# One causal attention layer of a decoder: both norms worked by batches inside the attention's stage, and the reciprocals of the softmax sums on ScalarE as exponential of the logarithm

## The reference, cut to what matters

```
x = x + L3_attn(layernorm(x))            # the first norm has no gain and no bias

def L3_attn(x, Wq, bq, Wk, bk, Wv, bv, Wo, bo, gamma, beta):      # 16 heads of 8
    q, k, v = heads(x @ Wq + bq), heads(x @ Wk + bk), heads(x @ Wv + bv)
    att = softmax(where(causal, q k^T / sqrt(8), -inf))
    y = merge(att v) @ Wo + bo
    return (y - mean(y)) / sqrt(var(y) + 1e-5) * gamma + beta     # the output norm
```

## Time and profile before

| | |
|---|---|
| median of 3 runs | 2105.82 us |
| profiled execution | 2109.4 us, span 2107.6 us, mean granted clock 0.949 |
| TensorE matmul, weight load | 1887.7 us (90%), 1342.2 us (64%) |
| VectorE, ScalarE, GpSimd | 1378.9 us (65%), 1159.7 us (55%), 897.8 us (43%) |
| `L2624` maxima, VectorE, in the layer | 57.3 us of 48 and 37.1 us of 32 |
| `L2607` exponentials, ScalarE, in the layer | 31.0, 24.4, 17.4 and 10.7 us, 32 of each width |
| `L2644` RECIPROCAL, VectorE | 26.9 us of 8, 3357 ns each |

### The profile page before, as it was taken

One profiled execution on the slowest core, in us unless ns is written; L12 is line 12 of the kernel. 1 busy time (PEld: TensorE's weight loads), 2 busy tenths in 40 slices (PEclk: granted clock), 3 DMA queues, 4 the chain that ended last, 5 costly groups with the idle time before them and its releaser, 6 DMA issues. The chain is left out here.

```text
span 2107.6 us, 50657 instructions
## 1 busy us (share of the span) xinstructions
PE 1887.7 (90%) x20016; PEld 1342.2 (64%) x20016; DVE 1378.9 (65%) x2444; ACT 1159.7 (55%) x2448; POOL 897.8 (43%) x1143
## 2 busy tenths in 40 slices
PE   7888999987568999999999877999899989999786
PEld 4336778853345788888888744888788856633332
DVE  4446788865944777777785334888777758934434
ACT  4555555555757666656664344555455551066453
POOL 0003445520625677666764201676566640044200
PEclk9999999999569999999999898999999999999898
DMA  6000100100003000000000042444344410000100
GB/s 290 1 1 2 61 30 31 41 1 0 1 0 151 33 14 23 14 23 14 23 17 20 23 181 53 123 130 135 108 127 127 130 41 2 1 1 1 37 1 21
DMA packets 31950, 107.00 MB, mean 51 GB/s; under 512 B 9440, under 2 KB 9568, under 8 KB 30816
## 3 DMA queue, kind: packets, MB, share of 16 engines
q1 hardware_dynamic: 30624, 103.58, 14.6%
q10 hardware_dynamic: 1088, 0.13, 0.0%
HBM read 93.67 MB, written 10.03 MB: 49 GB/s over the span
## 5 line engine op out<-in xcount | busy, mean ns | idle before, releaser
L762 PE MATMUL bank<-yh,wl 128*128 128x512 f32 x640 | 253.7, 396 | 11.7 <-issue 5.8
L763 PE MATMUL bank<-yl,wh 128*128 128x512 f32 x640 | 251.5, 393 | 0.0
L764 PE MATMUL bank<-yh,wh 128*128 128x512 f32 x640 | 251.5, 393 | 0.0
L2294 DVE SCALAR_TENSOR_TENSOR big<-bank,pack,big 128x256 f32<-128x256 f32 (+2 forms) x384 | 182.8, 477 | 40.2 <-ACT mask L2184 22.8
L1757 DVE TENSOR_TENSOR hl<-bank,hh 128x512 fp32r<-128x512 f32 x192 | 132.7, 691 | 69.3 <-ACT hh L1690 59.9
L2183 ACT ACTIVATE big<-bank,pack 128x256 f32<-128x256 f32 x192 | 91.1, 474 | 129.4 <-PE bank L1992 126.2
L1690 ACT ACTIVATE hh<-bank 128x512 fp32r<-128x512 f32 x192 | 115.0, 599 | 77.8 <-DVE bank L1752 77.7
L762 PEld LDWEIGHTS bank<-yh,wl 128*128 128x128 f32 x640 | 121.4, 190 | 47.1 <-issue 11.4
L754 POOL CAST wh<-big 128x384 fp32r<-128x384 f32 x64 | 62.1, 970 | 193.2 <-PE bank L764 132.1
L850 ACT ACTIVATE a<-bank,pack 128x512 f32<-128x512 f32 x128 | 88.1, 688 | 100.6 <-PE bank L764 100.6
L1588 POOL TENSOR_TENSOR a<-a,rep 128x512 f32<-128x512 f32 x96 | 126.1, 1313 | 31.4 <-DMA rep<-routing 27.1
(11 more groups left out here) (542 smaller groups left out, 4651.6 us busy)
## 6 DMA issues: line engine op xcount, KB each, us to landing
rep<-routing SPq DMA_DIRECT2D x64, 384.0 KB, 3.4
rep<-routing SPq DMA_DIRECT2D x64, 256.0 KB, 3.9
big<-in_big SPq DMA_DIRECT2D x1, 9216.0 KB, 25.4
rep<-routing SPq DMA_DIRECT2D x16, 512.0 KB, 3.6
gate<-big SPq DMA_DIRECT2D x32, 256.0 KB, 2.0
z<-gate SPq DMA_DIRECT2D x16, 512.0 KB, 3.5
rep<-routing SPq DMA_DIRECT2D x64, 128.0 KB, 3.6
big<-in_big SPq DMA_DIRECT2D x1, 6144.0 KB, 34.1
```

Source lines behind the costliest of these rows:

```text
L762: nc.tensor.matmul(out, pl, dh[:, cur], start=start, stop=False)
L763: nc.tensor.matmul(out, ph, dl[:, cur], start=False, stop=False)
L764: return nc.tensor.matmul(out, ph, dh[:, cur], start=False, stop=stop)
L2294: ins = nc.vector.scalar_tensor_tensor(out=d, in0=conv_in(i, back), scalar=weight(i, 3 - back), in1=d, op0=ALU.mult, op1=ALU.add)
```

## The change

The two calls of `norm` go, and their steps become steps of the attention's stage, placed in the engines' lists by batch. The first norm of batches 0 and 1 stands ahead of the first projection. For batches 2 and 3 `centre` stands behind look 5 and `variance` behind look 7 of batches 0 and 1; `square` and `invert` (Ln, Exp) follow on ScalarE behind the copies of the next batch, and `normed` stands behind maximum 8 on VectorE. The output norm of a batch follows its projection: `out_centre` at tile 10, `out_square` with a copy to `a` at tile 11, `out_variance` at tile 2 of the batch after (tile 14 of the same batch for batch 2), `out_invert` at tile 3, `scale_out` on VectorE at tile 6. That of batch 3 comes at the end. The reciprocal of the sums leaves `divide`; ScalarE does it in `invert_sums` as Ln and Exp with scale -1, at tiles 5 and 13. The new steps use banks 6, 7, 0 to 3 and buffers that are free at the time.

```diff
...
-    norm(nc, k, x, y, 1e-5)
-    causal_attention(nc, k, y, a)
-    norm(nc, k, a, y, 1e-5, scaled=(k.w["L3_attn_gamma"], k.w["L3_attn_beta"]), onto=x)
-
-
-def causal_attention(nc, k, y, a):
+    causal_attention(nc, k, x, y, a)
+
+
+def causal_attention(nc, k, x, y, a):
...
+            def centre(b):
+                if b >= 2:
+                    pe.wait_ge(s["q_out"], GROUPS * b)
+                nc.tensor.matmul(xc[b], k.w["centre"], x[:, sl(b)], start=True, stop=True).then_inc(s["centred"], 1)
+
+            def variance(b):
+                pe.wait_ge(s["squared"], b + 1)
+                if b >= 2:
+                    pe.wait_ge(s["k_out"], b)
+                nc.tensor.matmul(var[b], k.mean, sq[b % 2], start=True, stop=True).then_inc(s["var"], 1)
+
+            def out_centre(b):
+                pe.wait_ge(s["out"], b + 1)
+                nc.tensor.matmul(k.ps[7], k.w["centre"], a[:, sl(b)], start=True, stop=True).then_inc(s["out_centred"], 1)
+
+            def out_variance(b):
+                pe.wait_ge(s["out_squared"], b + 1)
+                if b < 2:
+                    pe.wait_ge(s["q_shifted"], GROUPS * (b + 3))
+                elif b == 2:
+                    pe.wait_ge(s["inverted"], 7)
+                else:
+                    pe.wait_ge(s["weights"], 2 * B * UNITS)
+                nc.tensor.matmul(out_var[b], k.mean, out_sq[:, :], start=True, stop=True).then_inc(s["out_var"], 1)
+
             def project_qk(b):
+                pe.wait_ge(s["y_ready"], b + 1)
                 pe.wait_ge(s["v_out"], b)
...
                 pe.wait_ge(s["q_out"], GROUPS * (b + 1))
+                if b in (1, 2):
+                    pe.wait_ge(s["y_ready"], b + 2)
                 for t in range(TB):
...
                 after(pe, s["out"], half // 2)
+                after(pe, s["out_kept"], half // 2)
+                if half % 2:
+                    after(pe, s["out_ln"], half // 2)
                 nc.tensor.matmul(k.ps[7], k.w["sum_rows"], raw[half % 2], start=True, stop=True).then_inc(s["shifted"], 1)
...
                 nc.tensor.matmul(k.ps[7], k.w["L3_attn_Wo_high"], o[1], start=False, stop=True).then_inc(s["proj"], 1)
+            centre(0)
+            centre(1)
+            variance(0)
+            variance(1)
             project_qk(0)
             project_v(0)
+            pe.wait_ge(s["y_ready"], 2)
             pe.wait_ge(s["consts"], 2)
...
                         project_qk(b + 1)
+                    if b < 2 and n == 5:
+                        centre(b + 2)
+                    if b < 2 and n == 7:
+                        variance(b + 2)
                     if b + 1 < B and n == 10:
...
                     values(u - LAG)
+                if b in (2, 3) and m == 2:
+                    out_variance(b - 2)
                 if b and m == 4:
...
                     project_out(b - 1)
+                if b in (1, 2, 3) and m == 10:
+                    out_centre(b - 1)
                 if b < B and m == 12:
                     shift_sums(2 * b)
+                if b == 3 and m == 14:
+                    out_variance(2)
                 if b + 1 < B and m == 15:
                     turn_most(b + 1)
+            out_centre(B - 1)
+            out_variance(B - 1)
         @block.scalar
...
+            def invert_sums(half):
+                act.wait_ge(s["shifted"], half + 1)
+                after(act, s["proj"], half // 2)
+                nc.scalar.activation(o[half % 2], k.ps[7], ACT.Ln).then_inc(s["sums_ln"], 1)
+                act.wait_ge(s["sums_ln"], half + 1)
+                nc.scalar.activation(o[half % 2], o[half % 2], ACT.Exp, scale=-1.0).then_inc(s["inverted"], 1)
+
+            def out_square(b):
+                act.wait_ge(s["out_centred"], b + 1)
+                after(act, s["out_var"], b)
+                nc.scalar.activation(out_sq[:, :], k.ps[7], ACT.Square).then_inc(s["out_squared"], 1)
+                if b + 1 < B:
+                    nc.scalar.activation(out_xc[b], k.ps[7], ACT.Copy).then_inc(s["out_kept"], 1)
+
...
+            square(0)
+            square(1)
+            invert(0)
+            invert(1)
             act.wait_ge(s["consts"], 1)
...
                     own_keys(b)
+                if b in (1, 2):
+                    square(b + 1)
+                    invert(b + 1)
             for u in range(B * UNITS):
+                b, m = divmod(u, UNITS)
                 w = (TB - u % TB) * P
...
                     nc.scalar.activation(dst, src, ACT.Exp, scale=-1.0).then_inc(s["weights"], 1)
+                if b in (2, 3) and m == 3:
+                    out_invert(b - 2)
+                if b and m == 5:
+                    invert_sums(2 * b - 1)
+                if b and m == 11:
+                    out_square(b - 1)
+                if m == 13:
+                    invert_sums(2 * b)
+            out_invert(2)
+            invert_sums(2 * B - 1)
+            out_square(B - 1)
+            out_invert(B - 1)
         @block.vector
...
             def divide(half):
-                dve.wait_ge(s["shifted"], half + 1)
-                after(dve, s["proj"], half // 2)
-                nc.vector.reciprocal(o[half % 2], k.ps[7]).then_inc(s["inverted"], 1)
                 dve.wait_ge(s["inverted"], half + 1)
...
+            def scale_out(b):
+                dve.wait_ge(s["out_rooted"], b + 1)
+                nc.vector.scalar_tensor_tensor(out=out_rs[:, :], in0=out_xc[b], scalar=k.w["L3_attn_gamma"], in1=out_rs[:, :],
+                                               op0=ALU.mult, op1=ALU.mult).then_inc(s["scaled"], 1)
+                dve.wait_ge(s["scaled"], b + 1)
+                nc.vector.scalar_tensor_tensor(out=x[:, sl(b)], in0=out_rs[:, :], scalar=k.w["L3_attn_beta"], in1=x[:, sl(b)],
+                                               op0=ALU.add, op1=ALU.add).then_inc(s["done"], 1)
+
+            normed(0)
+            normed(1)
             add_rows(0)
...
                     most(b, n)
+                    if b < 2 and n == 8:
+                        normed(b + 2)
                     if b + 1 < B and n == 11:
...
                     nc.vector.tensor_copy(raw[half % 2], k.ps[6]).then_inc(s["copied"], 1)
+                if b == B and m == 3:
+                    scale_out(2)
                 if b and m == 4:
                     divide(2 * b - 1)
+                if b in (2, 3) and m == 6:
+                    scale_out(b - 2)
                 if b and m == 9:
...
                     own_keys(b + 1)
-            dve.wait_ge(s["out"], B)
+            scale_out(B - 1)
+            dve.wait_ge(s["done"], B)
```

More of the change, by code:

```diff
@@ L2430, in causal_attention @@
     names = ("consts zeroed q_ps q_out k_ps k_out v_ps v_out k_own k_own_late v_spread scores most m_ready m_turned q_shifted "
-             "turned weights kept summed copied shifted inverted divided proj out")
+             "turned weights kept summed copied shifted inverted divided proj out "
+             "centred squared var ln rooted y_ready sums_ln out_centred out_squared out_kept out_var out_ln out_rooted scaled done")
     with ExitStack() as mem, stage(nc, names) as (block, s):
@@ L2441, in causal_attention @@
         own, spare, scale = k.w["own_head"], k.w["spare_row"], k.w["own_scaled"]
+        xc, var = (k.ps[0], k.ps[1], k.ps[6], k.ps[6]), (k.ps[2], k.ps[3], k.ps[7], k.ps[7])
+        out_xc = [a[:, sl(b)] if b + 1 < B else k.ps[7] for b in range(B)]
+        out_var = [k.ps[7] if b + 1 < B else k.ps[0] for b in range(B)]
+        sq, rs = ([pt[n][:, sl(d)] for d in range(2)] for n in range(2))
+        out_sq, out_rs = y[:, sl(0)], y[:, sl(1)]
         both = lambda n: k.all_ps[:, 2 * (n % 3) * S:(2 * (n % 3) + 2) * S]
@@ L2587, in own_keys, with square, invert, out_invert @@
                     nc.scalar.activation(kj[b][:, sl(j)], kd[b], ACT.Identity, scale=own[:, j:j + 1], bias=spare[:, j:j + 1]).then_inc(s["k_own"], 1)
+            def square(b):
+                act.wait_ge(s["centred"], b + 1)
+                after(act, s["var"], b - 1)
+                nc.scalar.activation(sq[b % 2], xc[b], ACT.Square).then_inc(s["squared"], 1)
+            def invert(b):
+                act.wait_ge(s["var"], b + 1)
+                after(act, s["y_ready"], b - 1)
+                nc.scalar.activation(rs[b % 2], var[b], ACT.Ln, bias=k.eps[1e-5]).then_inc(s["ln"], 1)
+                act.wait_ge(s["ln"], b + 1)
+                nc.scalar.activation(rs[b % 2], rs[b % 2], ACT.Exp, scale=-0.5).then_inc(s["rooted"], 1)
+            def invert_sums(half):
[10 more added lines that the diff above has]
+                    nc.scalar.activation(out_xc[b], k.ps[7], ACT.Copy).then_inc(s["out_kept"], 1)
+            def out_invert(b):
+                act.wait_ge(s["out_var"], b + 1)
+                after(act, s["scaled"], b)
+                nc.scalar.activation(out_rs[:, :], out_var[b], ACT.Ln, bias=k.eps[1e-5]).then_inc(s["out_ln"], 1)
+                act.wait_ge(s["out_ln"], b + 1)
```

(10 more changed lines are left out.)

## The result

The changed kernel takes 2130.1 us, the median of 20 runs (2104.36 to 2142.57), and the kernel before 2106.36 (20 runs, 2099.22 to 2131.75). The ratio is 1.0066, 95% interval 1.004 to 1.0093: +14 us on 2106, where +7.1 was forecast. On the 2105.82 us from which the forecast was reckoned that is 2119.7: inside the stated range of 2099 to 2122, above the forecast's own 2108 to 2118. The median of the 20 runs, 2130.1, lies above both.

The account below looks back on a forecast made before the run. Bound taken as waiting chains in opening and close, VectorE and TensorE in turn in the scores, TensorE in the weights. Terms -6.2 + 6.2 + 14.4 - 7.3 = +7.1 us gave 2112.9 us, range 2099 to 2122.

Parts of the forecast that it names:

- third rival: Granted clock falls in the middle: one 13.5 us stretch at half clock, +13.9 us in all, 2119.7; chance 17%.
- Opening: Layer start, up to the scores: two batches' norms, a stage boundary and constants leave the path, -6.2 us.
- Scores part: Added norm steps of batches 2 and 3 lengthen batches 0 and 1 by 3.08 us each, +6.2 us.
- Weights part: Added output norm matmuls 5.8, ScalarE's reciprocals 7.7 and one bank wait 0.96 us, sum +14.4 us.
- A pair: Weights part: each Ln and Exp behind tile 5 or 13 delays TensorE by 1.28 us, six cost 7.7.
- A matmul: Weights part: each of six out_centre and out_variance matmuls costs TensorE its full 0.96 us, 5.8 together.
- out_variance(2): Last weights batch, tile 13: TensorE waits 0.96 us ahead of this matmul for its bank.
- Close: Layer end: projection starts 2.0 us earlier and the chain to the last store shortens, -7.3 us in all.
- signs of being wrong: Weights batch 0 or scores batch 0 no longer than before, or a 1.2 GHz stretch in the middle of the weights.
- ScalarE hides the pairs: Weights part: Ln and Exp reciprocals cost nothing as ScalarE has free time; sum -1.5 us, 2104.3; chance 17%.

Follow-up runs that it names:

- best_early: Kernel best with centre, variance and scaling of batches 2 and 3 back at looks 5, 7 and maximum 8; +7 us against best at equal clock.
- pair_at_7: Changed kernel with tile 5's Ln and Exp pair moved behind tile 7's exponentials; -2.1 us against the changed kernel at equal clock.
- recip_vector: Changed kernel with the first seven half-batches' reciprocals back on VectorE, the last on ScalarE; -6.5 us against the changed kernel at equal clock.
- pairs_only: Kernel before with only the sums' reciprocals moved to ScalarE as Ln and Exp, norms in their own stages; +9.4 us against before at equal clock.
- late_norm: Changed kernel with centre and variance behind looks 14 and 16, scaling behind the last maximum; -6.1 us against the changed kernel at equal clock.
- after_again: The changed kernel unaltered, run again; +4.0 us against the kernel before at equal clock, mean clock 0.943.
- values_later: Changed kernel with the next batch's value projection behind look 12, not 10, its addition behind maximum 13; 2.5 us over the changed kernel's level, clock 0.936.
- vector_delay: Kernel before with four idle VectorE products behind maximum 8 of scores batches 0 and 1; +3.3 us at equal clock, mean clock 0.940.
- best: recip_vector and late_norm together, with batch 2's out_variance in bank 4 at the end; -11.2 us against before at equal clock, ratio 0.9979.
- best_again: Kernel best once more, unaltered; -10.6 us against the kernel before at equal clock, ratio 0.9935.

## Why the prediction was right, and where it was not

The sign and the place of most terms held. The change in time, +14 us, is twice the forecast +7.1, and the sum hid two misses in opposite directions: the work came to about +4 us, less than forecast, and about +10 us are the clock, of which the forecast had nothing. The stated range holds 2119.7 only because it was drawn over the third rival, whose own figure was also 2119.7. That the two agree is luck, as the rival took the full +7.1 of work and one low stretch of 13.5 us in the weights part.

- *Opening*, forecast -6.2, measured -9.0. The path was read rightly, but in the profile before it stood at 1.2 GHz for 10 us, and the forecast took the norm's pace over from there: the first Ln came 5.49 us after the layer's first matmul (1714.88 to 1720.37), in the changed kernel's profile at 2.4 GHz 3.07 us (1710.64 to 1713.71). Like with like, best_early's opening with 9 us at 1.2 GHz takes 15.7 for 21.1, so -5.4.
- *Scores part*, forecast +6.2. Batches without low clock take 30.8 for 27.7 (batch 0 of pair_at_7) and 30.3 for 27.2 (batch 1 of best_early): +3.1 each, the forecast's 3.08. Right as work.
- *Weights part*, forecast +14.4. A pair costs 1.15, forecast 1.28: right, and it is the position (recip_vector, pair_at_7). A matmul costs 0.5, forecast 0.96: the term that was mis-sized. Batch 1 of recip_vector has one (out_centre) and takes 32.0 for 31.5, batch 2 two and 32.6. With the 0.89 of out_variance(2) that makes an estimate of 10.8 us of work. TensorE did have a gap there that busy time hides. In the kernel before, tile 11's second score matmul waited for tile 10's first exponential. The values of tile 8 behind it start a new sum in bank 6, so they waited for VectorE's copy of that bank (L2667, done at 1928.73). The profile names GpSimd's cut for this second wait, but by the program tile 8 needs only its own cuts, long done. From the row of tile 11's score matmuls to the values it took 0.98 us; in the changed kernel the same step takes 0.43, because out_centre stands ahead and exponential and copy finish beside it:

```profile
1927.90 0.89 PE L2517 MATMUL bank<-big 32*128 32x128 f32 x8
1928.04 0.69 DVE L2667 COPY big<-bank 128x512 f32<-128x512 f32 x1 [0.28 <-PE bank L2531]
...
1928.88 1.07 PE L2531 MATMUL bank<-pt,vj 128*32 128x512 f32 x8
```

```profile
1981.24 1.13 PE L2494 MATMUL bank<-a,pack 128*128 128x512 f32 x2
1981.38 0.69 DVE L2785 COPY big<-bank 128x512 f32<-128x512 f32 x1 [0.28 <-PE bank L2563]
...
1982.30 0.50 PE L2549 MATMUL bank<-big 32*128 32x128 f32 x8
...
1982.73 1.06 PE L2563 MATMUL bank<-pt,vj 128*32 128x512 f32 x8
```

- *Close*, forecast -7.3, measured -7.8: right.
- *Sum at equal clock*: +4.2 and +4.0, forecast +7.1. The opening and the matmuls are off in that direction; the fit, which doesn't know where the low clock falls, can't divide it further.
- *The clock*, the third rival, was given 17% and is the larger part: the mean clock is 0.006 lower, 10 us by the fitted slope. The rival looked for it in the weights part, behind the pairs. That happened, and it is one of the prediction's own signs of being wrong: one or two stretches of 3 to 7 us at 1.2 GHz stand in weights batches 1 to 3 of each of the five profiles that have a pair at tile 5 (changed, pairs_only, late_norm, after_again, values_later), and in none of the other seven. It is the smaller share. A batch with 4 us of it takes 35.9 for 34.3 without (batch 1 of changed and of after_again), and pairs_only's mean clock, 0.949, is that of before within what 12 runs can tell. The larger share, which no part of the forecast had, is in the scores part: 36 us at 1.2 GHz in the changed kernel's profile, where the kernel before has 2.
- *What lowers it in the scores part* is shown in part. The clock fell amid the scores in the profiles of the five kernels whose early steps went ahead of the fall (changed, recip_vector, pair_at_7, after_again, values_later) and of vector_delay, and in none of late_norm, best, best_again, pairs_only and before; the mean clocks of the runs agree. vector_delay has no matmul more, so the added matmuls are not needed for it. values_later removed one of TensorE's pauses and others came, with a lower clock still. Open: why best_early did not fall after its early steps, whether it is TensorE's pauses or something else in a late VectorE, and what brings the third low stretch, in which nothing was added.
- *ScalarE hides the pairs*, the first rival: refused by recip_vector and pair_at_7. The Trainium skill (Perfetto Trace Analysis, Identifying the Most-Contended Engine) calls ScalarE's occupancy a fair measure of how close it is to its roofline. That the pairs therefore cost nothing was the prediction's reading of it, and this case's runs speak against that reading: ScalarE was a third idle, but only 0.06 us ahead of TensorE.

## What to carry to other kernels

Before moving work onto an idle engine, look at which instruction stands behind it in that engine's list, and how long before its reader it is done: here a third of free time and 0.06 us of slack cost 1.15 us a time, and two tiles further the same pair cost nothing. Where two engines take turns, put added work where the other one is the bound; a stage in which TensorE is nearly saturated can lose more through the clock than by the added work itself, as here with some 10 us against 4. And compare such kernels by many runs with their clocks, since single runs differ by more than the change.

## What the hardware showed that was not expected

In the changed kernel and in vector_delay TensorE's clock amid the scores first fell to 1.2 GHz after a stretch in which TensorE was busy 92 to 94% of the time (25.00 of 26.70 and 17.81 of 19.40 us above), with waits of 0.4 to 1.4 us. It then stayed there for 17 and 27 us although TensorE was busy without a gap (17.10 of 17.10 and 27.30 of 27.30 us).

The busy share alone does not tell when it falls. In the weights part the changed kernel's TensorE was busy 93% of a stretch (59.98 of 64.50 us) that stayed at 2.4 GHz. `best`, busy 98% in the scores part (103.57 of 105.40 us), did not fall. But vector_delay, busy 98% as well (16.32 of 16.70 us, with two waits of 0.2 us), fell for another 34.10 us, and so did recip_vector and after_again at the same place (each after 16.52 of 16.90 us). All three had been low twice shortly before, and the changed kernel, low twice too, did not fall there. What decides is open.
